# Low-key one-hots by comparisons with a scalar per tile, and the third product on ScalarE, in a two-layer graph network

## The reference, cut to what matters

```python
def _L0(node_features, edge_index, edge_features, W1, b1, W2, b2, U1, c1, U2, c2):
    h = relu(concatenate([node_features[src], edge_features]) @ W1 + b1)
    aggregated = segment_sum(h @ W2 + b2, dst)
    g = relu(concatenate([node_features, aggregated]) @ U1 + c1)
    return g @ U2 + c2

def _L1(x, eidx, enorm):
    return segment_sum(x[src] * enorm[:, None], dst)

h = maximum(layernorm(x), 0);  x = x + _L0(h, ...)
h = maximum(layernorm(x), 0);  x = x + _L1(h, ...)
```

## Time and profile before

| | us |
|---|---|
| median of 3 runs | 2448.67 (2445.86 to 2454.11) |
| the profiled execution | 2431.01 |
| its span, first to last instruction | 2429.2 |
| GpSimd busy in it | 1703.7 |
| TensorE busy | 1904.6 |
| VectorE busy | 1580.8 |
| ScalarE busy | 951.0 |

### The profile page before, as it was taken

How to read it: one execution, slowest core, us unless ns; L and a number is a source line. 1 busy time by engine, 2 the same in 40 slices (tenths; PEclk the granted TensorE clock), 3 DMA queues, 4 the chain that set the end, 5 groups by cost and what they waited for, 6 DMA issues and landing times.

```text
span 2429.2 us, 54571 instructions
## 1 busy us (share of the span) xinstructions
PE 1904.6 (78%) x19815; PEld 1568.8 (65%) x19815; DVE 1580.8 (65%) x4958; ACT 951.0 (39%) x2318; POOL 1703.7 (70%) x1663
## 2 busy tenths in 40 slices
PE   5766577667867787778778878888887988898898
PEld 5545455555655665667667767767776877777776
DVE  6856567666766666666666766667766766765443
ACT  3334344344444434434444444444444444442111
POOL 7777777777777777777777777777777777773000
PEclk9988888888888898889889989999999999998999
DMA  3345546544854684478358738857774775665897
GB/s 91 116 149 172 172 152 208 187 162 142 258 181 131 201 271 144 125 223 274 118 179 241 231 103 236 236 156 208 218 211 120 217 210 150 176 193 151 260 292 223
DMA packets 533582, 454.81 MB, mean 187 GB/s; under 512 B 296946, under 2 KB 485346, under 8 KB 527168
## 3 DMA queue, kind: packets, MB, share of 16 engines
q1 hardware_dynamic: 480516, 395.61, 52.1%
q0 software_dynamic: 52064, 53.17, 8.9%
q10 hardware_dynamic: 732, 2.48, 0.4%
HBM read 278.99 MB, written 172.09 MB: 186 GB/s over the span
## 4 chain that ended last, share of the span: by engine, by line
POOL 67%; issue 20%; PE 6%; DMA 4%; DVE 1%; SPq 0%; ACT 0%; POOLq 0%; ACTq 0%
POOL rows L729 67%; DMA stage<-adjacency 3%; PE pair L1162 2%; PE pair L974 1%; DMA x_all<-in_x_dram 1%; PE pair L1169 1%; PE pair L1176 1%; PE pair L1077 0%; PE pair L962 0%; PE pair L1063 0%; SPq L592 0%; DVE mean L1271 0%; PE pair L1184 0%; PE pair L1092 0%; DMA rows<-table,idx 0%
## 5 line engine op out<-in xcount | busy, mean ns | idle before, releaser
L729 POOL DMA_INDIRECT rows<-table,idx x1616 | 1656.1, 1025 | 509.1 <-issue 492.2
L842 ACT COPY stage<-pair 128x300 f32<-128x300 f32 x1616 | 622.9, 414 | 700.5 <-PE pair L1063 696.7
L1063 PE MATMUL pair<-bld 128*128 128x300 bf16 x4848 | 811.2, 325 | 4.7 <-DVE bld L1482 4.5
L1063 PEld LDWEIGHTS pair<-bld 128*128 128x128 bf16 x4848 | 568.0, 122 | 194.4 <-issue 32.2
L1035 PE MATMUL pair<-w1b,rings 128*128 128x128 f32 x1616 | 294.6, 339 | 456.2 <-DVE rings L1452 456.0
L1035 PEld LDWEIGHTS pair<-w1b,rings 128*128 128x128 f32 x1616 | 253.3, 238 | 504.6 <-DVE rings L1452 503.7
L1452 DVE TENSOR_TENSOR rings<-rows,pair 128x512 f32<-128x512 f32 x202 | 138.6, 686 | 524.2 <-DMA rows<-table,idx 523.4
L1482 DVE TENSOR_TENSOR bld<-bld,part 128x512 bf16<-128x512 bf16 x1212 | 432.6, 409 | 0.0
L1478 DVE TENSOR_SCALAR bld<-iota_key,key 128x300 bf16<-128x300 f16 x1616 | 387.0, 301 | 0.0
L834 ACT ACTIVATE rings<-rings 128x512 f32<-128x512 f32 x202 | 127.9, 633 | 364.5 <-DVE rings L1452 364.3
L1476 DVE TENSOR_TENSOR bld<-iota_lo,lo 128x512 bf16<-128x512 f16 x404 | 170.2, 421 | 139.9 <-PE pair L1063 135.3
(11 more groups left out here) (157 smaller groups left out, 1080.6 us busy)
## 6 DMA issues: line engine op xcount, KB each, us to landing
late_piece<-adjacency SPq DMA_DIRECT2D x207, 480.0 KB
rings<-in_edge_attr_dram SPq DMA_DIRECT2D x202, 256.0 KB
stage<-adjacency SPq DMA_DIRECT2D x72, 480.0 KB, 5.0
adjacency<-stage SPq DMA_DIRECT2D x28, 1200.0 KB
rows<-table,idx POOLq DMA_INDIRECT x1616
adjacency<-stage SPq DMA_DIRECT2D x20, 1080.0 KB
adjacency<-stage SPq DMA_DIRECT2D x20, 960.0 KB
adjacency<-stage SPq DMA_DIRECT2D x20, 840.0 KB
```

What stands on the lines that cost most here:

```text
L729: pool.indirect_dma_start(out=rows[:, slot, t, :], out_offset=None, in_=table, in_offset=bass.IndirectOffsetOnAxis(ap=idx[:, g, t:t + 1], ...
L842: act.copy(tiles[:, g % STAGE, :, t * WT:(t + 1) * WT], build_bank[i % 3][:, 0:KEYS].rearrange("p (h w) -> p h w", w=WT)).then_inc(tile_ke ...
L1063: last = pe.matmul(build_bank[i % 3][:, 0:KEYS], hot_w[q % 2][k][:, :, u], hot_key[q % 2][:, u, :], start=(k == 0), stop=(k == PARTS - 1))
```

## The change

`hot_eq` of a quad is made by four comparisons, each of 128 low keys with one scalar per partition (the low key of the tile's edge), written at a step of four elements, in place of the one comparison of 512 elements with a second tensor. `iota_lo` is one row of 128 instead of 128 by 4. The products with `part[0]` and `part[1]` stay on VectorE; those with `part[2]` are made by ScalarE in `weigh_last`, as four activations of 128 elements per quad, with the weight as a scale per partition, read from a small f32 copy (`far_now`, once per group). TensorE waits for `far_made` beside `quad_made`, and VectorE waits for `far_made` of quad q - 2 before it writes `hot_eq` again. ScalarE's first step waits for `w_split`.

```diff
@@ scalar @@
+            def weigh_last(q):
+                g, t = q // 2, q % 2 * 4
+                if t == 0:
+                    act.copy(far_now[:, g % TWO, :], part[PARTS - 1][:, g, :]).then_inc(far_moved, 1)
+                act.wait_ge(eq_made, q + 1)
+                act.wait_ge(far_moved, g + 1)
+                wait_count(act, tile_built, 4 * (q - 1))
+                for u in range(4):
+                    last = act.activation(hot_w[q % 2][PARTS - 1][:, :, u], hot_eq[q % 2][:, :, u], ACT.Copy,
+                                          scale=far_now[:, g % TWO, t + u:t + u + 1])
+                last.then_inc(far_made, 1)
...
                 act.wait_ge(table_turned, 20)
+                act.wait_ge(w_split, 5)
                 keep_eaT(0, 0, ea_bank)
+                weigh_last(0)
                 keep_eaT(1, 1, ea_bank)
+                weigh_last(1)
...
                             keep_eaT(s + 2, s % TWO, ea_bank)
+                        if s + 1 < GROUPS:
+                            weigh_last(2 * s + 2)
+                            weigh_last(2 * s + 3)
@@ tensor @@
                     pe.wait_ge(quad_made, q + 1)
+                    pe.wait_ge(far_made, q + 1)
@@ vector @@
                 wait_count(dve, tile_built, 4 * (q - 1))
-                dve.tensor_tensor(hot_eq[q % 2], iota_lo[:, :, :], over(lo[:, g, t:t + 4], P), ALU.is_equal).then_inc(eq_made, 1)
+                wait_count(dve, far_made, q - 1)
+                for u in range(4):
+                    last = dve.tensor_scalar(hot_eq[q % 2][:, :, u], iota_lo[:, :], lo[:, g, t + u:t + u + 1], None,
+                                             ALU.is_equal)
+                last.then_inc(eq_made, 1)
...
-                for k in range(PARTS):
+                for k in range(PARTS - 1):
                     last = dve.tensor_tensor(hot_w[q % 2][k], hot_eq[q % 2], over(part[k][:, g, t:t + 4], P), ALU.mult)
```

More of the change, by code:

```diff
@@ L293, in build @@
         hot_sum = sb("hot_sum", [P, TWO, W])
+        far_now = sb("far_now", [P, TWO, T])
         key_now = sb("key_now", [P, T])
@@ L316, in build @@
         iota_key = sb("iota_key", [P, KEYS], F16)
-        iota_lo = sb("iota_lo", [P, P, 4], F16)
+        iota_lo = sb("iota_lo", [P, P], F16)
         assert STAGE * ROW + 2 * COLS + 2 * QCOLS <= 10 * GE
@@ L435, in build @@
         quad_made = sem("quad_made")
+        far_made = sem("far_made")
+        far_moved = sem("far_moved")
         tile_built = sem("tile_built")
@@ L706, in _ @@
                       allow_small_or_imprecise_dtypes=True).then_inc(iotas_set, 1)
-            pool.iota(iota_lo[:, :, :], [[1, P], [0, 4]], base=0, channel_multiplier=0,
+            pool.iota(iota_lo[:, :], [[1, P]], base=0, channel_multiplier=0,
                       allow_small_or_imprecise_dtypes=True).then_inc(iotas_set, 1)
```

## The result

The changed kernel takes 2542.64 us (median of 4, 2536.66 to 2558.99), the kernel before in the same comparison 2447.27 us: 1.0415 times as long, with a 95% interval of 1.0372 to 1.0458. The forecast was 2397 us, and 2367 to 2432. It is 4.2% slower, not 2.1% faster.

A forecast was written before the change was run, and what follows sets the result against it. The prediction took GpSimd's back-to-back gathers, stretched by VectorE, as the bound. Saved 60 us less 8 paid gave 52 us, 2448.7 to 2397 us; own range 2369 to 2414, 8-in-10 range 2367 to 2432.

The forecast's parts named there:

- What bounds: GpSimd's 1616 gathers, one after another, set the time from 65.6 to 2214.0 us; a gather's duration is the lever.
- The product and L1476 leave VectorE, saved 60 us: In the one-hot building on VectorE, instructions that can hold a gather shrink from four to two per quad: saves 45 to 83.
- Four comparisons of 128 come in, paid 8 us: New VectorE comparisons at a step of four, 0.20 to 0.38 us each, hardly hold gathers; nearest row L1478 cost 5 us.
- Rival 2: New comparisons hold the port like the products: slower by 6 to 65 us, 2455 to 2514, likely near 2465; chance 0.07.
- Position: Gathers near VectorE's run, repriced by place for two products, keep 50 us: saved 61; 17 just ahead lose 0.67 us each.
- rival 1: Gathers fall into step with the shorter product run as badly as before: within 0.3%, about 2445 us; chance 0.07.
- ScalarE: Nine more instructions per step, activations about 0.27 us, up to 0.38: 1.8 to 2.7 us more per group.
- Waits, head and end phase: TensorE's and VectorE's new waits cost 0; head and end phase untouched, except the last group ends up to 2 us later.
- the pace of 10.2 us: Eight gathers per group at 1.28 us each, against TensorE's slow round of 10.4 to 10.9 us.
- Rival 3: The round through ScalarE and TensorE takes over and part of the gain is lost: about 2430 us; chance 0.08.
- a mean gather above 1010 ns: Sign in the profile after that the forecast is wrong; gathers over L1501 would tell whether comparisons hold them.

## Why the prediction was wrong, point by point

- **What bounds** was right: the gathers, one after another, before and with the change (67% and 70% of the chain), so the loss is theirs. Of the other kernels at the usual speed only the two with twelve fused comparisons are bound mostly by VectorE.
- **The product and L1476 leave VectorE, saved 60 us**: right in sign, too large, and lost in the whole. The third product alone away saved 131 - 100 = 31 us of stretches and 1.3% of the time. No run takes L1476 away alone.
- **Four comparisons of 128 come in, paid 8 us**: this is the step that failed. It took L1478 as the nearest row, "also a comparison with a scalar", and L1478 writes in order. VectorE's own time was sized well: 0.20 us in a row, the lower bound. What was wrong is that the comparisons hardly hold a gather: written at a step of four, they hold one until their chain ends. Alone, in place of L1476, they raised the stretches from 131 to 311 us and the time by 6.9%; in the whole change the stretches are 247 us, where the forecast left 131 - 52 = 79. Directly that was 24 us (the gathers that they catch later) on top of 17 us which L1476 had cost too. The bounds named the case, but at the size of the second rival with a chance of 0.07.
- **Position**: the estimate for the run of two moved each gather of before to the same place at the shorter run. But the places come from the program itself. The short comparisons release a gather at a fixed time, and the next start falls 0.12 us ahead of the products: 17 gathers became 144 (129 and 15). Priced at 0.67 us each, they cost 0.87: the cluster starts 0.1 us earlier than the gathers that were priced (0.74 us where no short comparison follows), and in 68 of its 129 cases the next quad's short comparisons follow at once (0.92 us). 138 us in the group ahead of the products instead of 11 is the loss.
- **Rivals**: rival 1 had the mechanism of position, and stopped at "as badly as before". Rival 2 named the sign, with the comparisons as holders, and its range (2455 to 2514) ended 29 us short of the result. What happened is both in one, each making the other dearer, and neither had a case for that. Its argument against, L1478's 5 us, was true of L1478.
- **The rule of the Trainium skill** ("SBUF — State Buffer", "Who interferes with whom") is that of VectorE in a two-port mode and GpSimd, whichever issues first has the shared pair for the whole instruction. The short comparisons at a step held gathers as that would have it; in order, 4848 of them cost some 4 us. The section doesn't make that distinction, and no run here shows in which mode a comparison ran. Of an instruction with two inputs in SBUF the section says less than the prediction does: that it contends with a GpSimd instruction that reads SBUF. The trace agrees, with 292 gathers that lost 93 us at L1482.
- **ScalarE**: 565 ns per activation, 1.5 times the upper bound (0.38), and it cost nothing visible: GpSimd never waited. **Waits, head and end phase**: nothing on the path, as forecast. But the pace of 10.2 us, against which the round over ScalarE was held, was too short: 8 gathers of 1.025 + 0.305 us are 10.6 us, and 10.4 with the forecast mean. Rival 3 had less for it than it seemed.
- Of the signs listed, the one that spoke was a mean gather above 1010 ns, with the gathers over L1501 to tell the rival.

## What to carry to other kernels

Where gathers issued back to back by GpSimd are the bound, VectorE's instructions are to be judged by whether they hold a gather back, not by how long they take: here a kernel whose one-hots keep VectorE busy for 1516 us instead of 990 is 2.4% faster. That has its limit, which the same kernel reaches: VectorE is then the bound itself, and its own time counts again. A nearest row must agree in the access pattern of its output, not only in operation and size. And where two engines hold each other up in a loop, positions are not random: two pieces in the other order moved the same kernel from 4.2% slower to 2.2% faster than before, so an estimate that averages over positions needs a range of both signs.

## What the runs showed of the hardware that was not expected

- A gather can be held by VectorE at two moments. One is at its start: 129 gathers that started 0.12 us ahead of a product were held, and none of the 40 that started 0.15 to 0.20 us ahead of one in the kernel before. The other is about 0.5 us in (the gather of 1150.03).
- Comparisons with a scalar, f16 in and bf16 out: written in order, chains of up to 16 leave gathers at 957 ns on the mean; written at a step of four elements, 1099 ns. In a row they start 0.223 us apart in order and 0.256 at the step.
- With a reduction of one element, 0.14 us, between the key comparisons and the products, 119 gathers that started up to 0.10 us ahead of the products lost nothing; without it 15 lost 0.75 us each. All stretches fell from 247 to 123 us.
- ScalarE's activation of 128 bf16 columns took 565 ns at a step of four in input and output and 387 ns in order; the copy of 300 f32 columns 415.
